# Two GELUs of the odd phases placed in one stop of ScalarE, with the work around them moved

## The reference

```python
x = L0_attn_x
xn = _layernorm(x, axis=-1)
return x + attn_stack(xn) + moe_ffn(xn)

# attn_stack: 4 layers, 16 heads of 8, 1024 positions in each of 2 batch rows
for i in range(4):
    n = layer_norm(x, ln1_w[i], ln1_b[i])
    x = x + mha(n, causal_and_alibi_mask, ...)      # softmax(q k / sqrt(8) + mask) v, then out_proj
    n = layer_norm(x, ln2_w[i], ln2_b[i])
    x = x + gelu(n @ ffn1_w[i].T + ffn1_b[i]) @ ffn2_w[i].T + ffn2_b[i]   # 128 -> 512 -> 128, exact gelu
return layer_norm(x, final_w, final_b)

# moe_ffn: 8 experts, top 2 of the router per token
for e in range(8):
    out += (gelu(xn @ w1[e] + b1[e]) @ w2[e] + b2[e]) * gate[:, e]
```

## Time and profile before

| | us |
|---|---|
| three runs | 1510.15, 1509.77, 1496.3 |
| median | 1509.77 |
| profiled execution, its own time | 1494.97 |
| its span, first to last instruction | 1493.2 |
| TensorE busy / VectorE busy / ScalarE busy / POOL busy | 1258.0 / 990.1 / 880.3 / 379.4 |
| mean granted TensorE clock | 0.937 |

### The profile page before, as it was taken

One profiled execution on the slowest core, in us unless ns is written; L12 is line 12 of the kernel. 1 busy time (PEld: TensorE's weight loads), 2 busy tenths in 40 slices (PEclk: granted clock), 3 DMA queues, 4 the chain that ended last, 5 costly groups with the idle time before them and its releaser, 6 DMA issues.

```text
span 1493.2 us, 30375 instructions
## 1 busy us (share of the span) xinstructions
PE 1258.0 (84%) x12316; PEld 632.6 (42%) x12316; DVE 990.1 (66%) x2112; ACT 880.3 (59%) x1115; POOL 379.4 (25%) x569
## 2 busy tenths in 40 slices
PE   3688788889988998888898999988989899888864
PEld 2333344444544445443544444434544444434323
DVE  5687566566676677757666687756666677766733
ACT  2046465665656676665656667665665766666652
POOL 4143611221213220321203120311213130022561
PEclk9589899998989999999999999999999999999998
DMA  8211522303323231403323041411324122211210
GB/s 245 78 46 59 155 73 70 105 28 103 112 70 102 62 108 44 128 17 106 104 74 106 20 136 34 121 63 60 105 77 132 35 76 95 64 39 40 57 53 14
DMA packets 108875, 120.19 MB, mean 80 GB/s; under 512 B 12096, under 2 KB 95168, under 8 KB 108736
## 3 DMA queue, kind: packets, MB, share of 16 engines
q1 hardware_dynamic: 100288, 90.38, 19.6%
q0 software_dynamic: 8448, 27.88, 6.6%
HBM read 78.63 MB, written 40.89 MB: 80 GB/s over the span
## 4 chain that ended last, share of the span: by engine, by line
PE 59%; DVE 21%; POOL 6%; issue 6%; ACT 6%; DMA 1%; SPq 1%; POOLq 0%; DVEq 0%; ACTq 0%
PE PS L1009 16%; DVE mx L1223 14%; PE PS L974 12%; PE PS L991 6%; PE PS L931 5%; PE PS L914 3%; PE PS L918 3%; PE PS L955 3%; PE PS L934 3%; PE PS L979 2%; PE PS L997 2%; ACT PR L801 2%; POOL w1G L624 1%; DVE st L1114 1%; POOL w2G L633 1%
## 5 line engine op out<-in xcount | busy, mean ns | idle before, releaser
L1223 DVE TENSOR_REDUCE mx<-PS 128x1 f32<-128x512 f32 (+3 forms) x1280 | 765.6, 632 | 346.0 <-PE PS L979 231.5
L801 ACT ACTIVATE PR<-PS 128x1024 f32<-128x1024 f32 (+3 forms) x768 | 606.0, 809 | 444.9 <-PE PS L997 276.8
L974 PE MATMUL PS<-Kop,Qop 64*128 64x512 bf16 (+3 forms) x1536 | 435.0, 346 | 118.3 <-DVE mx L1223 113.3
L991 PE MATMUL PS<-Qop,Kop 64*128 64x512 bf16 (+3 forms) x1536 | 349.2, 337 | 14.8 <-ACT PR L801 12.9
L1009 PE MATMUL PS<-PR,vbuf 128*32 128x512 f32 (+3 forms) x3072 | 341.6, 518 | 0.6 <-ACT PR L801 0.4
L974 PEld LDWEIGHTS PS<-Kop,Qop 64*128 64x128 bf16 x1536 | 130.9, 95 | 427.2 <-DVE mx L1223 329.0
L979 PE MATMUL PS<-idb,mk 64*128 64x64 bf16 x2048 | 191.0, 195 | 0.0
L979 PEld LDWEIGHTS PS<-idb,mk 64*128 64x128 bf16 x2048 | 162.6, 98 | 50.5 <-issue 8.7
L997 PE MATMUL PS<-idb,mk 64*128 64x64 bf16 x2048 | 173.7, 194 | 0.0
L991 PEld LDWEIGHTS PS<-Qop,Kop 64*128 64x128 bf16 x1536 | 106.5, 95 | 114.4 <-ACT PR L801 59.5
L997 PEld LDWEIGHTS PS<-idb,mk 64*128 64x128 bf16 x2048 | 138.8, 97 | 29.0 <-issue 2.9
(11 more groups left out here) (103 smaller groups left out, 1111.0 us busy)
## 6 DMA issues: line engine op xcount, KB each, us to landing
Qop<-qst SPq DMA_DIRECT2D x64, 256.0 KB, 2.7
Kop<-kst SPq DMA_DIRECT2D x64, 256.0 KB, 3.1
kst<-parts SPq DMA_DIRECT2D x32, 256.0 KB, 2.6
qst<-parts SPq DMA_DIRECT2D x16, 384.0 KB, 2.5
kst<-parts SPq DMA_DIRECT2D x32, 128.0 KB, 2.4
qst<-parts SPq DMA_DIRECT2D x16, 256.0 KB, 2.7
Qop<-mrow SPq DMA_DIRECT2D x256, 3.0 KB
onum<-osb SPq DMA_DIRECT2D x256, 16.0 KB
```

What stands on the lines that cost most here:

```text
L801: act.activation(PR[:, c % 4, :, 0:n], PS[:, 2 * (c % 2):2 * (c % 2) + 2, 0:n], ACT.Exp)\
L974: last = pe.matmul(PS[:, 5 + k % 2, n * e:n * e + n], Qop[r, par, a, P * i:P * i + P], Kop[r, kb, a, 512 * c:512 * c + n], start=True, sto ...
L991: last = pe.matmul(PS[:, 2 * (c % 2) + j, 0:n], Kop[r, kb, a, P * kt:P * kt + P], Qop[r, par, a, q0:q0 + n], start=True, stop=not DIAG[t])
L1223: dve.tensor_reduce(mx[:, par, i, 2 * heads[0] + j:2 * heads[-1] + j + 1:2, c], PS[:, 5 + k % 2, 0:n * len(heads)].rearrange("p (h n) -> p ...
```

## The change

In the odd phases the GELU of chunk 2 moves from slot 60 to slot 75 and that of chunk 3 from slot 84 to slot 75, so that both stand one behind the other. The h pieces of chunk 2 come earlier (slots 52 to 58 in place of 54 to 61), those of chunk 3 too (68 to 73 in place of 77 to 84), y 2 later (79 to 82 in place of 65 and 66), y 3 at 90 to 93 in place of 89 to 91. The turn of the next unit's first maxima moves from slot 85 to 87, the reciprocal from 90 to 89. The pace of the third unit becomes even; that of the fourth has 14 steps in slots 75 to 77. SyncE issues the fourth group's row load in the third unit ahead of the output of the left half, and the store of group 2 at the end of the fourth unit just before that of group 3. POOL gathers w2G for the fourth group behind the split of the fourth unit's first maxima. The computation is the same.

```diff
--- before.py
+++ after.py
@@ -88,8 +88,8 @@
     "odd": dict(
         pace=("020111011110111111011110111111011111000311101111",
               "010010332110001111000201211011020110021020112011",
-              "000120211101100101121110001430110111000220000212",
-              "011001111211101001111000153110010111101110101300"),
+              "011111011111011111011111011111011111011111011111",
+              "001100044321011101101001110111101111011110011100"),
         contents=(
             ((1,), 'wo', 0, 2), ((2,), 'turn0', 1, 4), ((6,), 'ln2', 0, 14), ((8,), 'h', (0, 0), 17),
             ((9,), 'h', (0, 1), 19), ((11,), 'h', (0, 2), 23), ((12,), 'h', (0, 3), 25), ((13,), 'turn0', 0, 26),
@@ -97,13 +97,13 @@
             ((22,), 'h', (1, 1), 45), ((23,), 'h', (1, 2), 46), ((26,), 'h', (1, 3), 53), ((26,), 'turn1', 1, 53),
             ((27,), 'ln1', 0, 55), ((28,), 'q', 0, 56), ((29,), 'k', 0, 59), ((30,), 'v', 0, 60),
             ((32, 32, 32, 34), 'y', 1, 70), ((36,), 'turn1', 0, 76), ((41,), 'ln1', 1, 82), ((41,), 'q', 1, 82),
-            ((43,), 'k', 1, 86), ((44,), 'v', 1, 88), ((50,), 'turn2', 1, 101), ((52,), 'xt', 2, 104),
-            ((54,), 'h', (2, 0), 108), ((57,), 'h', (2, 1), 114), ((58,), 'h', (2, 2), 121), ((61,), 'h', (2, 3), 122),
-            ((62,), 'turn2', 0, 127), ((65, 65, 65, 66), 'y', 2, 132), ((73,), 'turn3', 1, 146), ((76,), 'xt', 3, 152),
-            ((77,), 'h', (3, 0), 155), ((79,), 'h', (3, 1), 158), ((83,), 'h', (3, 2), 167), ((84,), 'h', (3, 3), 168),
-            ((85,), 'turn3', 0, 170), ((89, 89, 90, 91), 'y', 3, 184),),
-        gelu=(13, 27, 60, 84), stats2=(2, 14), stats1=(21, 37),
-        recip=(90, 8), norm=(95, 13), hi=(31, 42), mid=(32, 54), final=(64, 71)),
+            ((43,), 'k', 1, 86), ((44,), 'v', 1, 88), ((50,), 'turn2', 1, 100), ((51,), 'xt', 2, 102),
+            ((52,), 'h', (2, 0), 104), ((54,), 'h', (2, 1), 108), ((56,), 'h', (2, 2), 112), ((58,), 'h', (2, 3), 116),
+            ((61,), 'turn2', 0, 122), ((66,), 'xt', 3, 132), ((68,), 'h', (3, 0), 136), ((70,), 'h', (3, 1), 140),
+            ((72,), 'h', (3, 2), 144), ((73,), 'h', (3, 3), 146), ((74,), 'turn3', 1, 148),
+            ((79, 80, 81, 82), 'y', 2, 164), ((87,), 'turn3', 0, 174), ((90, 91, 92, 93), 'y', 3, 186),),
+        gelu=(13, 27, 75, 75), stats2=(2, 14), stats1=(21, 37),
+        recip=(89, 8), norm=(95, 13), hi=(31, 42), mid=(32, 54), final=(64, 71)),
     "even": dict(
         pace=("201011111101010120102011111102202001011111012110",
               "000002321201111100011111110202010111110102021101",
@@ -508,6 +508,9 @@
                         wait_apart(sp, S["s_bias"], 4 * p + 4)
                         weights_B(0 if f is None else f + 1)
                         weights_F(0 if f is None else f + 1)
+                    if j == 2 and b == 1 and q is not None:
+                        wait_apart(sp, S["s_taken"], base + number(contents, "xt", 2) + 1)
+                        rows_in(group_of(3, b, f))
                     outputs(u, U, 0)
                     if j == 0 and f is not None and q is not None:
                         wait_apart(sp, S["s_taken"], base)
@@ -529,10 +532,9 @@
                             if j == 2:
                                 wait_apart(sp, c_stg[row][half], STG * (q + 1))
                             load((u + 2) % UN, par, (j + 2) % 4, half)
-                            if half == 0 and j == 2 and f is not None and b == 1:
-                                group_out(group_of(2, b, f), base + number(contents, "y", 2) + 1)
-                                rows_in(group_of(3, b, f))
                             if half == 0 and j == 3:
+                                if f is not None and b == 1:
+                                    group_out(group_of(2, b, f), base + number(contents, "y", 2) + 1)
                                 group_out(group_of(3, b, f), base + number(contents, "y", 3) + 1)
                     outputs(u, U, 1)
 
@@ -681,8 +683,6 @@
                         g = group_of(2 if b == 1 else 3, b, f)
                         weights_1(g, base)
                         weights_2(g, None)
-                    if j == 3 and b == 1 and q is not None:
-                        weights_2(group_of(3, b, f), base + number(contents, "y", 2) + 1)
                     if j == 0 and f is None:
                         wait_apart(pool, S["s_route"], 1)
                         wait_apart(pool, S["c_zero"], 16)
@@ -691,6 +691,8 @@
                         split_mid(2 * p + 2, row, 0)
                     if j < 3 or q is not None:
                         max_parts(U + 1, 1 - par, 0)
+                    if j == 3 and b == 1 and q is not None:
+                        weights_2(group_of(3, b, f), base + number(contents, "y", 2) + 1)
                     if j == 2 and b == 1 and q is not None:
                         weights_1(group_of(3, b, f), base + number(contents, "h", (2, 3)) + 1)
                     if j == 0 and f is None:
```

## The result

| | before | after |
|---|---|---|
| runs, us | 1510.15, 1509.77, 1496.3 | 1524.8, 1524.35, 1520.56 |
| median, us | 1509.77 | 1524.35 |
| profiled execution, us | 1494.97 | 1524.8 |
| its span, us | 1493.2 | 1522.9 |
| mean granted clock | 0.937 | 0.928 |

The account below looks back on a forecast made before the run. TensorE (84% busy) was taken as the bound, its clock falls as the sizeable gain. Third and fourth units: 79.4 + 1.0 stop + 1.4 w2G + 1.3 clock = 83.1 us per phase against 84.1; 5 us off the median, 1505; range 1487 to 1518.

Parts of the forecast that it names:

- its own two rivals: Everything fits, no clock falls (22%): 1484 or 1499 us; w2G wait replaces the stop, slower (16%): 1507 or 1522 us.
- SyncE at the end of the fourth unit: Near slot 93 group 2's store lands within 0.3 us of y 3's copy being otherwise ready; booked 0, bound 2 us.
- Clock: Merged bunch, broken by values and pairs, resembles the even stop; one 3.4 us fall per phase at 1.3 us, bounds 0, 5.2.
- The reciprocal's wait: End of fourth unit: VectorE waits 3 to 4.7 us for the reciprocal's sums, 0 to 0.5 us of it exposed.
- The merged stop at full clock: From slot 75 ScalarE's stop is covered but TensorE not filled; loss 1.0 us, bounds 0.8 and 2.7.
- The third unit: Without its stop and y 2, with the fourth group's turn and two h pieces more: 38.1 us.
- The w2G wait: At slot 90 TensorE waits 1.4 us for the fourth group's gather before y 3; bounds 0 and 3.8.
- The rival built on this wait: y 3 starts 3.8 us late at slot 90, clock falls 6.8 us; 12 us slower, 1507 or 1522; chance 16%.
- two loads less per odd phase: ScalarE is spared 7.7 us of table loads over three odd phases; nothing booked directly.

Follow-up runs that it names:

- e2: The kernel before with only group 2's store moved to the end of the fourth unit, just ahead of group 3's; ratio 1.015 to the kernel before.
- e10: e6 with turn3 of the next unit back at slot 85 and the reciprocal back at slot 90; ratio 0.996 to the kernel before.
- e6: e1 with an extra 384-column matmul, result unread, behind each of 13 maximum steps in the merged stop; ratio 1.002 to the kernel before.
- e9: The changed kernel unaltered, timed again as common reference beside e10 and e12; ratio 1.011 to the kernel before.
- e5: e1 with the GELU of chunk 2 cut to one column, the rest of it left out; ratio 1.007 to the kernel before.
- e12: The kernel before with extra matmuls, results unread, behind the 15 maximum steps in its two odd stops; ratio 0.995 to the kernel before.
- e1: The changed kernel with group 2's store issued early, right behind the left output of the fourth unit; ratio 1.014 to the kernel before.

## Why the prediction was wrong

The predicted 1505 us lay outside what came, the range's end of 1518 too, and the sign was wrong. The range also left out the ends that its own two rivals had been given, 1484 and 1522. By its own steps:

- **SyncE at the end of the fourth unit: booked 0, bound 2. This step failed first.** The order was seen, and that y 3's copy waits for group 2's landing; the 3.6 us from the reciprocal's end to the store's issue came as forecast. The landing's price did not: I took 2.7 us, the median of ten stores at all places; right behind the two operand loads it took 4.3, 5.9 and 4.2. The 3.1 to 4.2 us of group 3's stores at that place stood in the trace before. I expected 0.3 us between the two sides; they were 1.2, 4.3 and 2.6. And I let the cost end where VectorE goes on, while e2 shows that 4.6 us of waiting there cost 6.8, the rest by the clock that falls in it. In the changed kernel it is 11.4 us over the three phases by the traces of after and e10, or 3.8 per phase.
- **Clock: booked 3.4 us of low clock per phase, at 1.3.** It was 13.7, 6.8 and 13.7 us in the merged stop alone and 3.4 to 6.4 more at the end. The argument that a bunch broken by values and pairs keeps its clock is refuted; e6 shows that it took real work in the gaps. The worth of full clock, 7.2 us over slots 75 to 84, is 2.4 per phase, within the bound of 5.2. The argument had rested on two stretches of 3.4 us, 2.54 us busy and held, 2.19 and fell. Two other stretches of the same trace say the opposite of those two: behind the first the clock held, behind the second it fell for 6.8 us.

```profile
370.00:373.40 3.40, 2.13 (x18) 1.35 (x17) 2.82 (x5) 3.09 (x3) 1.09 (x2) 1.00 0.00 0
```
```profile
1110.00:1113.30 3.30, 2.56 (x25) 1.50 (x25) 3.30 (x6) 2.56 (x3) 0.00 (x0) 1.00 0.00 0
```

- **The reciprocal's wait: near in size, wrong in cover.** 3 to 4.7 us were forecast, 3.05, 2.51 and 2.44 came. But the 0 to 0.5 exposed was 1.91 of TensorE idle time in that phase, and slots 91 to 94 give 5.3 us for all three, part of it half clock.
- **The merged stop at full clock: 1.0 booked, 2.7 the upper bound.** e10's fourth units take 44.3 against the 41.4 forecast for their work, with waits of 0.28, 0.46 and 1.04 us before y 3 among it: 2.3 without those. Not all of it need be the stop's. Laying the steps out one by one (2.7) was the nearer estimate, and I had set it aside because it overstated the single stops. Their loss was probably hidden in the comparison with a unit that has its own stalls; no run shows that.
- **The third unit: 38.1 forecast, 39.8 measured**, at clock 1.00 as said. TensorE is idle 5.7 us there, against 2.6 in the unit without group work, so probably the even pace and the pieces wait for one another; which term was short I did not separate.
- **The w2G wait: 1.4 booked.** None in phases 1 and 3, 0.92 in phase 5, where y 3's first piece is 8.8 us behind the gather's first issue (1136.09):

```profile
1144.85 1.13 PE L936 MATMUL PS<-w2G,hb 128*128 128x128 f32 x8 [0.92 <-issue]
```

In phase 1 7.8 us were enough (415.90 to 423.72). TensorE began 0.4 us behind the gather's last packet there and 0.5 us in phase 5, so the 7.6 us to the last packet (7.4 and 8.3 here) and 0.3 us for its tail were near. The cover was longer than the 7.8 us taken: from y 2's last piece (ended at 414.83) to y 3's first were 8.9 us in phase 1. The rival built on this wait, the one that ended slower, had the sign right and the cause wrong. The 3.1 us that the confirmation after the last byte would have made of it, by the Trainium skill's "DMA: Bandwidth & Descriptors", section "Anatomy of one DMA — SWDGE (gpsimd) path", did not come in this trace: 0.92 was the most, and 1.35 in e9's.
- **Right:** two loads less per odd phase, worth nothing directly. ScalarE's share of the chain stayed at 6%, and e5 shows 1.7 us less of ScalarE changing no slot. What the merge itself is worth at full clock can be read from e10 and e12: third and fourth units 252.2 against 247.7 us, and equal times. With the clock held in both, the new plan brings nothing.

Summed again with the measured terms: 84.1 per phase in e10, store 3.8, clock 2.4, reciprocal 1.8, which gives 92.1; the changed kernel has 39.8 + 52.2 = 91.9 (275.8 over three), against 83.1 forecast. The 8.8 us between are the store 3.8, the reciprocal 1.8, the third unit 1.7, the clock 1.1 above its 1.3, and 0.5 of stop and w2G wait above their 2.4, to 0.1.

Open: how much of the early store's gain in the trace (9.5 us in e1 against after) the times show. Their intervals are 8 to 14 us wide, and e1's traced execution was the fastest of its four (1508.5 us, median 1516.2). e5, whose fourth units are as long as e1's (146.9 us), came at 1.007, against 1.011 for the changed kernel in e9; these intervals overlap too. Open as well: what sets the two levels of the kernel before, and why the clock falls for 6.8 us in one execution and 13.7 or 17.1 in another.

## What to carry to other kernels

When a store is moved behind others in a queue, ask which single buffer it frees and price its landing with the traffic that it will stand behind, not by the median of its kind. A wait that leaves TensorE idle can cost more than its length, by the clock that falls in it: 19.3 us for 12.9 in e2. Read a wait's length with care: of the 15.7 us put down to the store here, 7.5 would have been spent waiting for TensorE. Where TensorE is paced by another engine for some microseconds, look at its granted clock, and try cheap matmuls in the gaps before rearranging the plan; where the clock holds anyway, they cost time.

## What the runs showed of the hardware

- Thirteen matmuls of 384 columns, 0.34 us each, in the gaps of a stretch of 11.3 us kept the clock at 1.00 (e6) where it had been at 0.58 and 0.77 on average (e1, two phases). The stretch took 11.3 us with them, 11.5 to 13.2 without, where the clock fell each time; no run shows it without them at full clock.
- Low clock in the merged stop lasted 6.8, 13.7 or 17.1 us for the same instructions in the same order (after, e1, e9). Fourth units of e1 with 17.1 us of low clock in all took 50.1 and 50.3 us, the one with 6.8 took 46.5.
- The same 256 KB store took 2.7 us in the median and, right behind two 256 KB loads, 4.2 to 5.9 us in the changed kernel and 3.8 to 4.9 in e2.
